# Token-routed audio layer: the last two expert blocks joined by one-hot products of rounded halves, fetched rows summed on VectorE

## The reference

```python
logits = conv3(gelu(conv3(x)))                    # 10 experts, 896 tokens
vals, idx = top_k(logits, 2); gv = softmax(vals)  # two experts a token
gates[n, idx] = gv
h = elu(x @ e_w1[e] + e_b1[e])                    # 128 -> 512, per expert
y = sum_e gates[:, e] * (h @ e_w2[e] + e_b2[e])   # 512 -> 128
sh = conv1(silu(conv9(x)))                        # shared branch, 128 -> 512 -> 128, bias sh_b2
z = x + y + sh
out = tokens + layernorm(z) * ln_g + ln_b
```

## Time and profile before

| | |
|---|---|
| median of 3 runs | 160.23 us (159.71 to 160.25) |
| the profiled execution's own time | 159.43 us |
| its span, first to last instruction | 157.6 us |
| busy, share of span: PE, DVE, ACT, POOL | 94%, 81%, 48%, 56% |
| granted TensorE clock, mean | 0.994 of full speed |

### The profile page before, as it was taken

How to read it: one execution, slowest core, us unless ns; L and a number is a source line. 1 busy time by engine, 2 the same in 40 slices (tenths; PEclk the granted TensorE clock), 3 DMA queues, 4 the chain that set the end, 5 groups by cost and what they waited for, 6 DMA issues and landing times.

```text
span 157.6 us, 3090 instructions
## 1 busy us (share of the span) xinstructions
PE 148.3 (94%) x1015; PEld 133.8 (85%) x1015; DVE 127.8 (81%) x354; ACT 75.9 (48%) x201; POOL 88.4 (56%) x79
## 2 busy tenths in 40 slices
PE   7999879999998999999999999999999999999960
PEld 2699669999976639899999988999999999989830
DVE  0069999999998999879977666999999999892592
ACT  2324964211028779961044325677777777730030
POOL 3173899999999983005777700155544455552050
PEclk9999999999999999999999999999999999999997
DMA  5999999995970000000397129999998984001603
GB/s 142 336 410 404 239 188 279 212 117 100 175 125 4 0 0 4 0 0 17 96 304 292 53 69 292 388 398 376 283 340 293 335 285 188 33 33 31 223 0 116
DMA packets 19553, 28.30 MB, mean 180 GB/s; under 512 B 4838, under 2 KB 14193, under 8 KB 19538
## 3 DMA queue, kind: packets, MB, share of 16 engines
q1 hardware_dynamic: 16918, 21.42, 44.5%
q0 software_dynamic: 1696, 5.52, 14.5%
q10 hardware_dynamic: 924, 1.17, 2.4%
HBM read 19.67 MB, written 5.28 MB: 158 GB/s over the span
## 4 chain that ended last, share of the span: by engine, by line
PE 85%; DVE 7%; POOL 4%; issue 1%; ACT 1%; DVEq 0%; POOLq 0%
PE psum L713 17%; PE psum L624 14%; PE psum L753 13%; PE psum L741 13%; PE psum L521 4%; PE psum L532 4%; PE psum L856 4%; POOL prod L346 4%; PE psum L649 2%; PE psum L728 2%; PE psum L555 2%; DVE raw L1289 2%; PE psum L544 1%; PE psum L850 1%; PE psum L801 1%; PE psum L894 1%
## 5 line engine op out<-in xcount | busy, mean ns | idle before, releaser
L506 POOL DMA_INDIRECT ys_rows<-yb,xid x22 | 21.7, 986 | 25.6 <-ACT yb L1109 25.6
L1099 ACT ACTIVATE wu<-psum,wring 128x128 f32<-128x128 f32 x92 | 26.1, 369 | 11.3 <-PE psum L741 11.3
L1406 DVE SCALAR_TENSOR_TENSOR tb<-psum,wring,wu 128x128 f32<-128x128 f32 x92 | 25.9, 345 | 0.8
L753 PE MATMUL psum<-wring,tb 128*128 128x128 f32 x184 | 24.6, 277 | 0.0
L741 PE MATMUL psum<-xTb,wring 128*128 128x128 f32 x184 | 24.3, 275 | 0.0
L496 POOL DMA_INDIRECT xs_rows<-xT_s,slot x14 | 14.4, 1032 | 16.1 <-DVE slot L1338 12.1
L741 PEld LDWEIGHTS psum<-xTb,wring 128*128 128x128 f32 x184 | 22.3, 192 | 0.5 <-issue 0.5
L753 PEld LDWEIGHTS psum<-wring,tb 128*128 128x128 f32 x184 | 22.4, 192 | 0.4 <-DVE tb L1406 0.2
L624 PE MATMUL psum<-prod,ident_s 128*128 128x196 f32 (+1 forms) x120 | 21.6, 341 | 1.1 <-POOL prod L346 1.1
L624 PEld LDWEIGHTS psum<-prod,ident_s 128*128 128x128 f32 x120 | 21.1, 190 | 1.2 <-issue 1.2
L358 POOL TENSOR_TENSOR prod<-es,vt 128x3136 f32<-128x3136 f32 x3 | 19.4, 6462 | 0.2 <-ACT es L977 0.2
(11 more groups left out here) (180 smaller groups left out, 277.0 us busy)
## 6 DMA issues: line engine op xcount, KB each, us to landing
wring<-wexp SPq DMA_DIRECT2D x23, 514.0 KB, 5.2
wu<-raw POOLq DMA_DIRECT2D x2, 1536.0 KB, 12.1
raw<-wsh SPq DMA_DIRECT2D x2, 768.0 KB, 8.5
xs_rows<-zero_s SPq DMA_DIRECT2D x1, 1472.0 KB, 16.3
ys_rows<-zero_s SPq DMA_DIRECT2D x1, 896.0 KB, 22.9
xT_s<-xT SPq DMA_DIRECT2D x2, 384.0 KB, 5.4
wu<-wsh SPq DMA_DIRECT2D x1, 768.0 KB, 6.5
xb<-xs_rows SPq DMA_DIRECT2D x1, 585.0 KB, 6.4
```

Of the source, the lines that this page charges most:

```text
L506: pool.indirect_dma_start(ys_dram, bass.IndirectOffsetOnAxis(ap=xid[:, j:j + 1], axis=0), yb[:, j % NY, :], None)\
L753: ins = mm(ps[Y_BANK][:, 0:D], tb[:, j % NTT, c, :], wring[:, j % NR, W2 + c * P:W2 + (c + 1) * P], start=(c == 0), stop=(c == HC - 1))
L1099: ins = A(eb[:, j % NEB, c, :], ps[U_BANKS[j % NU]][:, c * P:(c + 1) * P], ACT.Exp, bias=wring[:, j % NR, B1 + c:B1 + c + 1])
L1406: ins = V.scalar_tensor_tensor(tb[:, j % NTT, c, :], ps[U_BANKS[j % NU]][:, c * P:(c + 1) * P], wring[:, j % NR, B1 + c:B1 + c + 1], eb[:, ...
```

## The change

1. **The last two blocks** (`LAST`, 21 and 22) are joined by products instead of only the last; POOL scatters one block fewer, and the fetches wait for one block fewer. ACT rounds each of the two `yb` to float32r (`y_high`), DVE subtracts to get the rest (`y_low`), and PE multiplies the zeros and ones, now float32r too, by both parts: 2 blocks x 7 tiles x 2 parts = 28 products of 128 columns.
2. **Block 21's down product** goes to another bank (`y_ps`), so it no longer waits until ACT has emptied the common one.
3. **The gate table** is transposed in one product of 77 columns, and the biases are added with one product for each part (K = 77; the bias table `b2sh` is 77 x 896 instead of 11 x 128, and is loaded later, behind the first four blocks of weights).
4. **z**: PE's two identity products of fetched rows for `TILES[0]` go, and so does its residual for `TILES[1]`. DVE instead sums the fetched rows of both parts (`fetched`), adds the residual for `TILES[1]`, and adds the PSUM bank at the end (`joined`). The first `shared_down` of the two parts change places.
5. **POOL** adds the shift `ln_b` to `h2` behind its last scatter; DVE did it before (line 1420).
6. **DVE's subtractions** in `low_part` and at line 1341 are `scalar_tensor_tensor` (with a product by 1.0) instead of `tensor_tensor`.
7. **PE** gets one more filling product (`keep_going(1, ...)`) between two of the first convolution products.

```diff
+LAST = (NB - 2, NB - 1)
...
+        hot = sb("hot", [P, len(LAST), NT, P], F32R)
+        y_last = sb("y_last", [P, len(LAST), 2, D], F32R)
...
+        def y_ps(j):
+
+            return ps[U_BANKS[NB % NU] if j == NB - 2 else Y_BANK][:, 0:D]
...
-            sp.dma_start(b2sh_s[:], b2sh).then_inc(S("ld_b2"), 16)
             sp.wait_ge(S("pool_cst"), 4)
...
             for j in range(EARLY):
                 load_weights(j)
+            sp.dma_start(b2sh_s[:], b2sh).then_inc(S("ld_b2"), 16)
             sp.wait_ge(S("scattered"), 16 * TOP * NT)
...
             for k in range(NY):
-                sp.wait_ge(S(f"ys_out{k}"), 16 * ((NB - 2 - k) // NY + 1))
+                sp.wait_ge(S(f"ys_out{k}"), 16 * ((LAST[0] - 1 - k) // NY + 1))
...
-                for j in range(a, min(b, NB - 1)):
+                for j in range(a, min(b, LAST[0])):
...
+            pool.tensor_tensor(h2[:], h2[:], rows_s[:, R_LNB:R_LNB + 1, :].broadcast_to([P, NT, D]), ALU.add).then_inc(S("h2_done"), 1)
             for done, k in enumerate((1, 0)):
...
                 pe.wait_ge(S("tb_done"), j + 1)
-                if j >= 1:
+                if j == 0:
+                    pe.wait_ge(S("y1_done"), HC)
+                elif j == NB - 2:
+                    pe.wait_ge(S("tb_done"), NB - NU)
+                else:
                     pe.wait_ge(S("yb_done"), j)
...
             with_high(0, 1)
+            keep_going(1, M_BANK[0][3])
             with_low(0, 1)
...
+            def second_bias(hf):
+
+                lo, hi = HALVES[hf]
+                mm(ps[Z_BANKS[hf]][:, 0:hi - lo], gatesT, b2sh_s[:, lo:hi], start=False, stop=False)
...
+            def last_blocks(hf):
+
+                for n, j in enumerate(LAST):
+                    pe.wait_ge(S("hot_done"), n + 1)
+                    pe.wait_ge(S("y_high"), n + 1)
+                    pe.wait_ge(S("y_low"), n + 1)
+                    for i in TILES[hf]:
+                        for part in range(2):
+                            ins = mm(z_ps[i], hot[:, n, i, :], y_last[:, n, part, :], start=False,
+                                     stop=(j == LAST[-1] and i == TILES[hf][-1] and part == 1))
+                ins.then_inc(S("z_mm"), 1)
...
-            for k, queue in enumerate(("sp", "act")):
-                pe.wait_ge(S(f"yg_{queue}0"), 16)
-                ins = mm(ps[Z_BANKS[0]][:, 0:len(TILES[0]) * D], ident_s[:], yg[:, k, TILE_RANGE[0], :], start=False, stop=(k == TOP - 1))
-            ins.then_inc(S("z_mm"), 1)
...
+            act.wait_ge(S("yb_done"), NB)
+            for n, j in enumerate(LAST):
+                A(y_last[:, n, 0], yb[:, j % NY, :], ACT.Copy).then_inc(S("y_high"), 1)
             for k in range(NY):
...
-                V.tensor_tensor(dsf_l[:, sl], dsf[:, sl], dsf_h[:, sl], ALU.subtract).then_inc(S("dsf_l"), 1)
+                V.scalar_tensor_tensor(dsf_l[:, sl], dsf[:, sl], 1.0, dsf_h[:, sl], ALU.mult, ALU.subtract).then_inc(S("dsf_l"), 1)
...
-            V.tensor_tensor(wu12_l[:, 1], wu12[:, 1], wu_h[:, 2], ALU.subtract).then_inc(S("wu2_l"), 1)
+            V.scalar_tensor_tensor(wu12_l[:, 1], wu12[:, 1], 1.0, wu_h[:, 2], ALU.mult, ALU.subtract).then_inc(S("wu2_l"), 1)
...
+            for n, j in enumerate(LAST):
+                V.scalar_tensor_tensor(hot[:, n], tok_t[:, n].rearrange("p (i o) -> p i o", o=1).broadcast_to([P, NT, P]), 1.0,
+                                       rows_s[:, R_PLACE:R_PLACE + 1, :].broadcast_to([P, NT, P]), ALU.mult, ALU.is_equal).then_inc(S("hot_done"), 1)
+                dve.wait_ge(S("y_high"), n + 1)
+                V.scalar_tensor_tensor(y_last[:, n, 1], yb[:, j % NY, :], 1.0, y_last[:, n, 0], ALU.mult, ALU.subtract).then_inc(S("y_low"), 1)
...
+            def fetched(hf):
+
+                sl = TILE_RANGE[hf]
+                dve.wait_ge(S(f"yg_sp{hf}"), 16)
+                dve.wait_ge(S(f"yg_act{hf}"), 16)
+                link(V.scalar_tensor_tensor(zt[:, sl, :], yg[:, 0, sl, :], 1.0, yg[:, 1, sl, :], ALU.mult, ALU.add))
...
+            def joined(hf):
+
+                sl = TILE_RANGE[hf]
+                dve.wait_ge(S("z_mm"), 2 - hf)
+                link(V.tensor_tensor(zt[:, sl, :], tiles3(ps[Z_BANKS[hf]], len(TILES[hf])), zt[:, sl, :], ALU.add))
...
+            fetched(1)
             sl = TILE_RANGE[1]
...
+            link(V.scalar_tensor_tensor(zt[:, sl, :], zt[:, sl, :], 1.0, x3[:, sl, :], ALU.mult, ALU.add))
+            fetched(0)
+            joined(1)
             ln_stats(3, zt_t, 1)
...
             less_mean(1, zt_t)
-            dve.wait_ge(S("z_mm"), 2)
-            ln_stats(3, z_ps, 0)
-            less_mean(0, z_ps)
+            joined(0)
+            ln_stats(3, zt_t, 0)
+            less_mean(0, zt_t)
```

More of the change, by code:

```diff
@@ L243, in build @@
         dm = sb("dm", [P, NT])
-        tok = sb("tok", [P, 2])
-        tok_t = sb("tok_t", [P, NT])
+        tok = sb("tok", [P, 2, len(LAST)])
+        tok_t = sb("tok_t", [P, len(LAST), NT])
         ed = sb("ed", [P, NT])
@@ L837, in _ @@
                     pe.wait_ge(S(done), c - 1)
[L838 removed]
+                    if c == 3 and m == 1:
                         pe.wait_ge(S("gT_done"), 1)
[L840 to L841 removed]
                     for part in range(3):
@@ L844, in _, with shared_down @@
                     if c == 2 and m == 2:
[L845 to L852 removed]
+                        gate_transpose()
+            def second_bias(hf):
+                lo, hi = HALVES[hf]
+                mm(ps[Z_BANKS[hf]][:, 0:hi - lo], gatesT, b2sh_s[:, lo:hi], start=False, stop=False)
+            def shared_down(hf, c, opens=False):
                 pe.wait_ge(S("tsh_done"), c + 1)
                 for i in TILES[hf]:
[L856 to L864 removed]
+                    mm(z_ps[i], tsh[:, c, i * P:(i + 1) * P], wsh2_s[:, c, :], start=(opens and i == TILES[hf][0]), stop=False)
+            def last_blocks(hf):
[8 more added lines that the diff above has]
+                ins.then_inc(S("z_mm"), 1)
             pe.wait_ge(S("y1_done"), HC - 1)
@@ L869, in _ @@
             residual(Z_BANKS[0], x3, TILES[0])
-            shared_down(0, 0)
             block_x(0)
             block_x(1)
-            residual(Z_BANKS[1], x3, TILES[1])
+            shared_down(1, 0, True)
             block_up(0)
@@ L879, in _ @@
                     block_up(step - 1)
-                else:
-                    second_bias(TILES[step - NB - 1])
                 if step == 3:
-                    shared_down(1, 0)
+                    shared_down(0, 0)
+                if step == NB + 2:
+                    second_bias(0)
                 if step >= 3:
                     block_down(step - 3)
+            second_bias(1)
             for hf in (1, 0):
@@ L901, in _ @@
                 pe.wait_ge(S("diag_done"), NT + n + 1)
-                ins = mm(r_ps[:, n * D:(n + 1) * D], xnT[:, n * P:(n + 1) * P], x1[:, i, :], start=False, stop=(i == TILES[1][-1]))
+                ins = mm(r_ps[:, n * D:(n + 1) * D], ex1[:, n * P:(n + 1) * P], x1[:, i, :], start=False, stop=(i == TILES[1][-1]))
             ins.then_inc(S("h2_mm"), 1)
@@ L1080, in _ @@
             first_sum(2)
-            for hf in (1, 0):
-                gates_in_rows(hf)
+            gates_in_rows()
             tanh(1)
@@ L1125, in _ @@
             for n, i in enumerate(TILES[1]):
-                A(xnT[:, n * P:(n + 1) * P], ident_s[:], ACT.Copy, scale=rstd[:, 3, i:i + 1])\
+                A(ex1[:, n * P:(n + 1) * P], ident_s[:], ACT.Copy, scale=rstd[:, 3, i:i + 1])\
                     .then_inc(S("diag_done"), 1)
@@ L1413, in _ @@
                 block_elu(step - 2)
-            last_id = xb[:, NB - 1, X_ID:X_ID + 1]
-            link(V.tensor_scalar(tok[:, 0:1], last_id, float(N), float(N), ALU.is_ge, ALU.mult))
-            link(V.tensor_tensor(tok[:, 1:2], last_id, tok[:, 0:1], ALU.subtract))
-            link(V.tensor_tensor(tok_t[:], tok[:, 1:2].broadcast_to([P, NT]), iota[:, IOTA_T:IOTA_T + NT], ALU.subtract))
-            V.tensor_tensor(hot, tok_t[:].rearrange("p (i o) -> p i o", o=1).broadcast_to([P, NT, P]),
-                            rows_s[:, R_PLACE:R_PLACE + 1, :].broadcast_to([P, NT, P]), ALU.is_equal).then_inc(S("hot_done"), 1)
@@ L1420, in _ @@
-            V.tensor_tensor(h2[:], h2[:], bc(R_LNB).broadcast_to([P, NT, D]), ALU.add).then_inc(S("h2_done"), 1)
-            sl = TILE_RANGE[1]
-            dve.wait_ge(S("z_mm"), 1)
-            dve.wait_ge(S("yg_sp1"), 16)
-            link(V.tensor_tensor(zt[:, sl, :], tiles3(ps[Z_BANKS[1]], len(TILES[1])), yg[:, 0, sl, :], ALU.add))
-            dve.wait_ge(S("yg_act1"), 16)
-            link(V.tensor_tensor(zt[:, sl, :], zt[:, sl, :], yg[:, 1, sl, :], ALU.add))
+            last_ids = xb[:, LAST[0]:LAST[-1] + 1, X_ID]
@@ new lines, in _ @@
+            link(V.tensor_scalar(tok[:, 0], last_ids, float(N), float(N), ALU.is_ge, ALU.mult))
+            link(V.tensor_tensor(tok[:, 1], last_ids, tok[:, 0], ALU.subtract))
```

(9 more changed lines are left out.)

53 lines of the change are left out of this document (14 added, 39 removed).

## The result

The changed kernel took 160.75 us (median, 159.87 to 162.27) where the kernel before took 159.95 (159.17 to 162.21) beside it: a ratio of 1.0046, 95% interval 1.0028 to 1.0065, so 0.74 us slower. (The ratio is taken over fast executions alone, so it differs a little from that of the two medians.) I had forecast 0.68 us faster. The profiled execution took 160.85 us, its span is 158.9. A line of the changed kernel has another number than before; the tiles' names tell which answers to which.

A forecast was written before the change was run, and what follows sets the result against it. PE bounds the kernel, with the scatter, fetch and DVE chain close behind. The loop runs 1.06 - 0.02 - 0.22 = 0.82 us sooner, statistics 0.68 sooner; 160.23 - 0.68 gives 159.6 us, eight-in-ten range 158.7 to 162.2.

The forecast's parts named there:

- The scatters lose their stretch: First two scatters on POOL: 1.64 and 1.23 us fall to 0.96 each, so xb lands 0.95 us sooner, at 93.67.
- The rival of the collision: First scatters: any DVE instruction reading two SBUF tensors stretches them, so the 0.95 us is lost; 160.5 us, chance 0.12.
- Gate transposes: PE ahead of block 0: six of seven transposes go at 0.11 us each, 0.65 us sooner on PE.
- The end on PE: PE's last products: all start 0.82 us sooner, and PE ends TILES[0] at 148.82 against 150.76 before.
- the operands: Inputs of the 28 products: first hot near 141.3, second with remainders near 143.1; PE wants them at 143.15 and 0.64 later.
- POOL's sum hidden: POOL's ln_b addition after the last scatter: about 2 us, near 139.4 to 141.4, covered because PE needs h2 after 148.8.
- the 0.20 that I had PE wait for block 22's ELU: PE before block 22's down product: previous products end at 139.40, its ELU at 139.60.
- Rounded products: PE's 28 products of 128 columns at the end: 0.107 us each, so 1.28 us for 12 and 1.71 for 16.
- The rival of dear ones: Narrow rounded products at the end cost 0.223 us each, a float32 product's price; 162.3 us, chance 0.20.
- Fetch: Fetch of rows at the end: SP issues at 141.05, last part lands between 145.6 and 146.3, taken as 146.0.
- DVE ends last: At the end DVE reaches the statistics of TILES[0] at 150.10, after PE is ready at 148.82, with 0.56 us between them.

The follow-up runs named there:

- e1: Changed kernel without the two DVE subtractions beside the first scatters, that part of the computation left out; ratio 0.9996 to the kernel before.
- e7: Changed kernel with those subtractions moved from beside the first scatters, partly to POOL, nothing left out; ratio 1.0002 to the kernel before.
- e2: Changed kernel with the same two subtractions cut into pieces of 256 columns, 4 and 6 instructions; ratio 1.0057 to the kernel before.
- e5: Changed kernel with the one gate transpose made seven times, same output; ratio 1.0050 to the kernel before.
- e3: Changed kernel with POOL's addition of ln_b held until both remainders of y are written; ratio 0.9999 to the kernel before.
- e6: Changed kernel with the two-column tok step made as two one-column steps, POOL's addition left in place; one execution, xb to statistics 56.73 us.
- e8: Changed kernel with subtractions moved from the scatters, POOL's ln_b addition behind both remainders, each bias product one block earlier; ratio 0.9979 to the kernel before.

## Why the prediction was wrong, by its steps

**The scatters lose their stretch: this step failed, and with it the sign.** The stretch stayed, whatever the form of the subtractions; e1 and e7 show that it is theirs. In place of the assumption that `scalar_tensor_tensor` doesn't collide the runs put: a scatter that starts while DVE runs an instruction with two SBUF inputs waits for it. It can be read off the rows: in the changed kernel the first scatter starts at 72.97 and DVE's next instruction at 73.53; 0.56 and the 1.13 of the undisturbed first scatter make 1.69, measured 1.64. The second starts at 74.92, DVE's next at 75.20: 0.28 + 0.99 = 1.27, measured 1.23. The evidence that I had held against this, a scatter of 0.96 beside a two-input line, started 0.02 us ahead of that line, and so was never held. I had compared durations and not starts. The kernel before had a row that spoke against it:

```profile
84.52 1.30 DVE L1371 SCALAR_TENSOR_TENSOR raw<-ex,xnT 128x256 f32<-128x256 f32 x4 [1.12 <-ACT ex L1063]
84.74 1.04 POOL L496 DMA_INDIRECT xs_rows<-xT_s,slot  x1 [0.30 <-issue]
```

This scatter started 0.22 us after the first of that line's four pieces, which are `scalar_tensor_tensor` already, and took 0.08 us more than the ordinary 0.96.

The Trainium skill, "SBUF — State Buffer", section "Who interferes with whom", has this rule for a VectorE instruction with two SBUF inputs against a GpSimd instruction that reads SBUF, with the first comer keeping the port for its whole length; these runs agree where VectorE's instruction came first, and e2's second scatter was held longer than one instruction. Where a scatter came first the runs differ from it, and show no wait: e7's subtraction of 640 columns took 0.80 us while a scatter ran, no more than the 1.22 for 1024 columns and 1.75 for 1536 would give. The Trainium skill's remark there that `tensor_tensor` was not seen to stall descriptor generation does not hold here: the kernel before has 1.64 beside one.

What it cost: `xb` came 22.08 us after the first scatter where the forecast had 22.20 - 0.95 = 21.25, so 0.83 of the gain was missing. The size of the term was about right: without the collision the same stretch is 21.45 (e1) and 21.30 (e7). The rival of the collision named this, with 0.12 and 160.5 us.

**Gate transposes: right in size, worth nothing.** PE's list got 0.64 shorter, and `xb` decided (e5).

**The end on PE: the operands did not come in time.** The forecast had PE done 148.82 - 93.67 = 55.15 us after `xb`; it was 149.24 + 1.98 - 95.05 = 56.17, 1.02 later. Nearly all of that lies behind the start of the 18 shared passes, which came 142.56 - 95.05 = 47.51 after `xb` where the forecast had 141.14 - 93.67 = 47.47. From there PE needed 8.66 us instead of 7.68, and without the held `tok` (e3) 149.22 + 1.98 - 143.27 = 7.93. I had the operands in time and POOL's sum hidden; in fact the sum held `tok` for 2 us, and PE lost 0.73 by it. Of the other 0.25, 0.20 are the rounded products (below). I had costed it by what waits for POOL, and not by what DVE shares with it. The rival's text had `hot` held 1.3 us at most and absorbed by PE; both are too little. e6 shows the way of it: one column passes, two columns do not, and a two-input instruction does not. By the Trainium skill, "VectorE: DVE Perf Modes", section "Mode 2×_2P — use both read ports for one tensor", a `tensor_scalar` in SBUF with an even count can take both read ports; the 2.03 us for two columns against 0.20 for two steps of one agrees.

A second wait, the 0.38 us (138.75 to 139.13) of block 21's down product for its ELU, was not forecast either: the change took away the bias products that stood between the earlier trace rows, and I counted the ELU of block 22 alone. That the 18 shared passes came on time all the same is luck: from `xb` to the end of block 20's down product the loop took 138.75 - 95.05 = 43.70 us where my sum had 137.65 - 93.67 = 43.98, and the 0.20 that I had PE wait for block 22's ELU went into the new wait. In e8, with the bias products earlier again, the same passes start 141.16 - 94.03 = 47.13 after `xb`, 0.38 sooner.

**Rounded products: right in kind.** The 12 take 1.37 us where nothing holds them (e3, 145.20 to 146.57) and the 16 take 1.82, where the forecast had 1.28 and 1.71: 0.114 each for 0.107, 0.20 together. The rival of dear ones is out. **Fetch: sooner than forecast.** SP issued it 141.94 - 95.05 = 46.89 us after `xb` (forecast 141.05 - 93.67 = 47.38), and its last part landed at 146.56, 51.51 after `xb` (forecast 52.33). That the clock time came near the forecast's 146.0 is luck, since `xb` was later. **DVE ends last: wrong**, since it waited 0.74 us for PE.

The sum: 0.83 missing at `xb`, and the stretch behind it 56.94 where the forecast had 150.10 - 93.67 = 56.43, 0.51 more. Together 1.34, which turns -0.68 into +0.66 in the trace; the runs have +0.74 and, the second time, 0.0034 x 160.5 = +0.55.

**What stays open.** Why e2's second scatter was held across three boundaries, and why the undisturbed first scatter takes 1.13 and not 0.96. The 0.38 wait was not undone by itself, only in e8, where PE shows no wait there; so no run shows what it alone is worth in device time.

## What to carry to other kernels

Where two engines share a port, read which of two instructions started first before you take a short row as evidence that they don't collide. Work given to GpSimd "because it idles" is costed by the VectorE instructions that run beside it, each with its number of SBUF inputs, and a tiny one on the critical path can lose the whole length of GpSimd's. And a saving on one engine is worth what the second chain leaves of it: here 0.65 us of products went into a wait of 1.28.

## What the hardware showed that I had not expected

- A `tensor_scalar` on 128x2 took 2.03 us beside a GpSimd `tensor_tensor` of 2.09, and 0.16 without it; on 128x1 twice, 0.20 beside it.
- A scatter started 0.33 us ahead of a two-input VectorE instruction was not lengthened (1.13 with and without); one started inside such an instruction took 1.64, and 2.24 inside a row of short ones.
- The first scatter of one kernel lay between 72.42 and 73.84 us in three executions, and the device times were 159.43, 159.37 and 161.55 us. Of the 2.12 us that the last took more than the first, 1.42 lay ahead of the first scatter.
